# Summing a graph layer's edges on 64-row tiles: six edges in a row on a partition instead of three

## The reference

```python
agg = segment_sum(edge_attr, dst, num_segments=6250)     # (6250, 128)
h   = relu(concat([x, agg, u[0]]) @ W1 + b1)              # (6250, 256)
y   = x + (h @ W2 + b2 + x)
out = layernorm(y)                                        # (6250, 128)
```

## Time and profile before

| | us |
|---|---|
| median of 3 runs | 177.22 (176.80 to 177.23) |
| the profiled execution, its own time | 177.16 |
| span of the profile | 175.4 |
| PE busy / its share of the span | 150.3 / 86% |
| DVE busy / share | 119.8 / 68% |
| ACT busy, POOL busy | 52.8, 34.3 |
| mean rate of the DMA engines | 354 GB/s over 62.07 MB |
| mean granted clock of PE | 0.991 of full speed |

### The profile page before, as it was taken

How to read it: one execution, slowest core, us unless ns; L and a number is a source line. 1 busy time by engine, 2 the same in 40 slices (tenths; PEclk the granted TensorE clock), 3 DMA queues, 4 the chain that set the end, 5 groups by cost and what they waited for, 6 DMA issues and landing times.

```text
span 175.4 us, 5350 instructions
## 1 busy us (share of the span) xinstructions
PE 150.3 (86%) x2191; PEld 113.1 (64%) x2191; DVE 119.8 (68%) x352; ACT 52.8 (30%) x109; POOL 34.3 (20%) x40
## 2 busy tenths in 40 slices
PE   0054799999999999997996999999989999999960
PEld 0044576866796786864774675976845976887840
DVE  5754388988586797766676462797875675685552
ACT  2002242334431430432330423224304305214430
POOL 7900030424120020020020020110200200019350
PEclk9999999999999999999999999999999999999996
DMA  4999999999999999999999999999999999999941
GB/s 110 302 371 382 377 382 376 371 384 372 372 383 373 372 384 371 373 381 375 369 381 374 379 376 372 380 374 374 378 375 373 375 370 371 373 372 384 371 178 37
DMA packets 42244, 62.07 MB, mean 354 GB/s; under 512 B 2023, under 2 KB 39589, under 8 KB 42218
## 3 DMA queue, kind: packets, MB, share of 16 engines
q1 hardware_dynamic: 41094, 61.23, 98.8%
q10 hardware_dynamic: 1124, 0.48, 1.2%
HBM read 58.50 MB, written 3.20 MB: 352 GB/s over the span
## 4 chain that ended last, share of the span: by engine, by line
PE 64%; DMA 23%; DVE 7%; ACT 2%; issue 2%; SPq 0%; DVEq 0%
PE sum_ps L903 22%; DMA edge_ring<-in_edge_attr_dram 20%; PE out_ps L995 9%; PE hid_ps L963 9%; PE hid_ps L976 8%; PE turn_ps L923 7%; DMA base_row<-in_dst_dram 3%; PE xt_ps L941 2%; DVE bases L640 2%; PE hid_ps L995 1%; PE keep_ps L976 1%; PE keep_ps L949 1%; DVE local_rows L648 1%; DVE agg_t L702 1%; ACT local_t L512 1%
## 5 line engine op out<-in xcount | busy, mean ns | idle before, releaser
L903 PE MATMUL sum_ps<-edge_ring,onehot 128*32 128x128 f32 x1662 | 56.7, 280 | 6.5 <-DMA edge_ring<-in_edge_attr_dram 4.2
L903 PEld LDWEIGHTS sum_ps<-edge_ring,onehot 128*32 128x32 f32 x1662 | 43.9, 111 | 14.8 <-DMA edge_ring<-in_edge_attr_dram 6.8
L702 DVE TENSOR_TENSOR agg_t<-agg_t,turn_ps 128x112 f32 x70 | 19.0, 272 | 42.5 <-PE turn_ps L923 38.1
L666 DVE TENSOR_TENSOR onehot<-iota,local_t 128x768 f32<-128x768 f32 (+1 forms) x37 | 42.2, 1142 | 2.4 <-ACT local_t L512 2.4
L469 POOL TENSOR_TENSOR x_all<-x_all,half_b 128x512 f32<-128x512 f32 (+3 forms) x16 | 18.0, 1136 | 113.4 <-PE xt_ps L941 113.4
L524 ACT COPY sums<-sum_ps 128x256 f32<-128x256 f32 (+2 forms) x37 | 13.3, 360 | 61.7 <-PE sum_ps L903 61.7
L923 PEld LDWEIGHTS turn_ps<-place,sums 128*128 128x128 f32 (+1 forms) x140 | 20.2, 191 | 11.1 <-issue 9.1
L923 PE MATMUL turn_ps<-place,sums 128*128 128x112 f32 (+1 forms) x140 | 21.4, 273 | 1.1 <-ACT sums L524 1.1
L976 PE MATMUL hid_ps<-agg_t,w_a 128*128 128x512 f32 (+1 forms) x48 | 22.0, 581 | 0.0
L995 PE MATMUL out_ps<-w_sb,hid_t 128*128 128x128 f32 x160 | 20.4, 281 | 0.0
L995 PEld LDWEIGHTS out_ps<-w_sb,hid_t 128*128 128x128 f32 x160 | 18.7, 191 | 1.8 <-issue 1.8
(11 more groups left out here) (78 smaller groups left out, 91.0 us busy)
## 6 DMA issues: line engine op xcount, KB each, us to landing
edge_ring<-in_edge_attr_dram SPq DMA_DIRECT2D x69, 768.0 KB, 12.0
x_all<-in_x_dram SPq DMA_DIRECT2D x10, 256.0 KB, 10.8
out_dram<-x_all SPq DMA_DIRECT2D x1, 2304.0 KB
dst_rows<-in_dst_dram SPq DMA_DIRECT2D x1, 384.0 KB
x_all<-in_x_dram SPq DMA_DIRECT2D x3, 128.0 KB, 10.9
out_dram<-x_all SPq DMA_DIRECT2D x3, 128.0 KB
out_dram<-x_all SPq DMA_DIRECT2D x1, 256.0 KB
w_x<-in_L_gnn_W_dram ACTq DMA_DIRECT2D x1, 128.0 KB, 6.1
```

Source lines behind the costliest of these rows:

```text
L666: nc.vector.tensor_tensor(onehot[0:ROWS, b % BUFFERS, 0:k * TILES], cols, loc, ALU.is_equal).then_inc(onehot_ready, 1)
L702: nc.vector.tensor_tensor(to, to, turn_ps[:, i * SPAN:(i + 1) * SPAN], ALU.add).then_inc(group_added, 1)
L903: last = nc.tensor.matmul(bank[c * WIN:(c + 1) * WIN], onehot[0:p, b % BUFFERS, i * TILES + c * R + r], edge_ring[0:p, slot, c * R + r], s ...
```

## The change

A partition now holds R = 6 edges in a row, and a window of 384 edges lies on one half of the partitions (64). A group is two blocks s of 128 partitions; the half h of block s is a window. The load of a group moves 256 runs of 3072 bytes. The one-hot matrices are the same in number and size. A sum is now a product over 64 rows: twice as many matmuls, each on a tile of 64 rows and 32 columns of PE. In the second group of a pair the two windows of a block go to swapped places (`to_swapped` gives the offsets to match), so that the two row halves which use the same column tile belong to different groups, and `sum_ps` has a bank for each group of the pair. The matmuls of both groups of a pair are issued in turn. All batches are pairs (35). The second bank comes from `keep_ps`, of which one is left: C_'s product with x is now kept in `x_hid_late` too, and the four products are made one after another in steps 5 to 8. The last pieces' outputs, norms and roots stand in another order.

```diff
-R = 3
+R = 6
 C = 4
-ROWS = 128
-TILES = C * R
+HALF = P // 2
+SUPER = 2
+TILES = SUPER * R
-EDGES_WIN = R * ROWS
+EDGES_WIN = R * HALF
-COMPLETE_AT = [6, 12, 18, 24, 30, 36, 40, 46, 52, 58, 60, 64, 66, 67, 68]
-SINGLE0 = 66
+COMPLETE_AT = [6, 12, 18, 24, 30, 36, 40, 46, 52, 58, 60, 64, 66, 68, 68]
-LATE_SUM_STEP = [5, 6, 7]
+LATE_SUM_STEP = [5, 6, 6, 7, 8]
...
-        sum_ps = psum("sum_ps", [P, BLOCK])
+        sum_ps = psum("sum_ps", [P, PAIR, BLOCK])
-        keep_ps = [psum(f"keep_ps{m}", [P, BLOCK]) for m in range(m_chunks)]
+        keep_ps = psum("keep_ps", [P, BLOCK])
...
-                    sp.dma_start(edge_ring[0:ROWS, slot].rearrange("p (c r) f -> p c (r f)", c=C),
+                    sp.dma_start(edge_ring[:, slot].rearrange("p (s r) f -> p s (r f)", s=SUPER),
                                  edges[g * EDGES_GRP:(g + 1) * EDGES_GRP, :]
-                                 .rearrange("(c p r) f -> p c (r f)", c=C, p=ROWS)).then_inc(...)
+                                 .rearrange("(s p r) f -> p s (r f)", s=SUPER, p=P)).then_inc(...)
...
+            nc.gpsimd.tensor_copy(by_swapped[:, :, 0], by_window[:, :, 1])
+            nc.gpsimd.tensor_copy(by_swapped[:, :, 1], by_window[:, :, 0]).then_inc(consts_ready, 1)
...
-                nc.scalar.copy(sums[0:w, b % 2, 0:k], sum_ps[0:w, 0:k * d].rearrange("s (k f) -> s k f", k=k)
-                               ).then_inc(batch_copied, 1)
+                if b < n_batch - 1:
+                    nc.scalar.copy(sums[:, b % 2], sum_ps[:, :, 0:d]).then_inc(batch_copied, 1)
+                    return
+                nc.scalar.copy(sums[:, b % 2, 0], sum_ps[:, 0, 0:d])
+                nc.scalar.copy(sums[0:WIN, b % 2, 1], sum_ps[0:WIN, 1, 0:d]).then_inc(batch_copied, 1)
...
             relu(END)
-            root(E)
-            root(END)
+            for n in range(C_, n_pieces):
+                root(n)
...
-            norm_step(E, 3)
-            norm_step(E, 4)
-            for step in range(5):
+            for step in range(3):
+                norm_step(ODD, step)
+            norm_step(C_, 3)
+            for step in range(3):
+                norm_step(E, step)
+            norm_step(ODD, 3)
+            for step in range(3):
                 norm_step(END, step)
+            for n in (E, END):
+                norm_step(n, 3)
+                norm_step(n, 4)
...
-            nc.tensor.matmul(out_ps[:, spread_at], to_window[:], rel_t[:, 0:n_grp], start=True,
+            nc.tensor.matmul(out_ps[:, win_at], to_window[:], win_row[:], start=True, stop=True)
+            nc.tensor.matmul(out_ps[:, spread_at], to_window[:], rel_t[:, 0:n_grp], start=True, stop=True)
+            nc.tensor.matmul(out_ps[:, swapped_at], to_swapped[:], rel_t[:, swapped], start=True,
                              stop=True).then_inc(rel_spread, 1)
...
-            def sum_group(b, i, g):
-                slot, bank = g % SLOTS, sum_ps[:, i * d:(i + 1) * d]
-                pe.wait_ge(edges_landed[slot], 16 * (g // SLOTS + (1 if g < full_grp else rest_wins + 3)))
-                for r in range(R):
-                    for c in range(C if g < full_grp else last_wins):
-                        ...
-                        last = nc.tensor.matmul(bank[c * WIN:(c + 1) * WIN],
-                                                onehot[0:p, b % BUFFERS, i * TILES + c * R + r],
-                                                edge_ring[0:p, slot, c * R + r],
-                                                start=(r == 0), stop=(r == R - 1))
-                last.then_inc(group_summed, 1)
+            def sum_window(b, i, g, s, h, r, p):
+                slot, rows_h = g % SLOTS, slice(h * HALF, h * HALF + p)
+                place_at = 2 * s + (h if i == 0 or g == full_grp else 1 - h)
+                return nc.tensor.matmul(sum_ps[place_at * WIN:(place_at + 1) * WIN, i, 0:d],
+                                        onehot[rows_h, b % BUFFERS, i * TILES + s * R + r],
+                                        edge_ring[rows_h, slot, s * R + r],
+                                        start=(r == 0), stop=(r == R - 1))
+
+            def sum_batch(b):
+                pe.wait_ge(onehot_ready, b + 1)
+                for g in groups(b):
+                    pe.wait_ge(edges_landed[g % SLOTS], 16 * (g // SLOTS + (1 if g < full_grp else 3)))
+                whole = [g for g in groups(b) if g < full_grp]
+                for r in range(R):
+                    for s in range(SUPER):
+                        for h in range(2):
+                            for i, g in enumerate(whole):
+                                last = sum_window(b, i, g, s, h, r, HALF)
+                                if (r, s, h) == (R - 1, SUPER - 1, 1):
+                                    last.then_inc(group_summed, 1)
+                if b == n_batch - 1:
+                    for r in range(R):
+                        last = sum_window(b, 1, full_grp, 0, 0, r, rest_rows + (r < rest_tiles))
+                    last.then_inc(group_summed, 1)
...
-            def sum_x_kept():
-                pe.wait_ge(x_t_ready, turned_at[A] + 1)
-                for m in range(m_chunks):
-                    nc.tensor.matmul(keep_ps[m][:, 0:2 * half], w1_x[:, m * P:(m + 1) * P], x_t_late[:, part_cols(0)],
-                                     start=True, stop=True).then_inc(late_x_summed, 1)
+            def sum_x_kept(k, m):
+                pe.wait_ge(x_t_ready, turned_at[late_parts[k][0]] + 1)
+                if k + m > 0:
+                    pe.wait_ge(late_x_kept, m_chunks * k + m)
+                cols = part_cols(0) if k == 0 else late_cols(C_)
+                nc.tensor.matmul(keep_ps[:, 0:cols.stop - cols.start], w1_x[:, m * P:(m + 1) * P], x_t_late[:, cols],
+                                 start=True, stop=True).then_inc(late_x_summed, 1)
...
+            sum_out(ODD)
             sum_hidden_a(END)
+            sum_out(E)
             sum_out(END)
```

More of the change, by code:

```diff
@@ L103, in gnn_resnorm_kernel @@
     pool_scaled = range(LAST, E)
-    assert all(a < b for a, b in zip(hidden_step, hidden_step[1:])) and hidden_step[END] == n_batch
+    assert all(a <= b for a, b in zip(hidden_step, hidden_step[1:])) and hidden_step[END] == n_batch
     made_by = [min(b + 3 + sum(hidden_step[n] <= b for n in range(AHEAD - 2)), n_batch) for b in range(n_batch)]
@@ L180, in gnn_resnorm_kernel @@
         x_t_late = sb("x_t_late", [P, n_nodes - late0])
-        x_hid_late = sb("x_hid_late", [P, m_chunks, 2 * half])
+        x_hid_late = sb("x_hid_late", [P, m_chunks, 3 * half])
         hid_t = sb("hid_t", [P, 2, m_chunks, BLOCK])
@@ L211, in hidden_bank @@
                 return hid_ps[m][:]
-            bank, at = {A: (hid_ps[0], 0), B: (hid_ps[1], 0), C_: (keep_ps[0], 0), ODD: (xt_ps, 0),
-                        E: (keep_ps[1], 0), END: ((xt_ps, 2 * P), (keep_ps[1], P))[m]}[n]
+            bank, at = {A: (hid_ps[0], 0), B: (hid_ps[1], 0), C_: (hid_ps[0], 0), ODD: (xt_ps, 0),
+                        E: (keep_ps, 0), END: ((xt_ps, 2 * P), (keep_ps, P))[m]}[n]
             return bank[:, at + m * p * j:at + (m + 1) * p * j]
@@ L511, in _ @@
                 t1 = min(t0 + per_bank, TILES)
-                last = nc.scalar.copy(lt[0:ROWS, t0:t1],
-                                      ps[0:ROWS, 0:(t1 - t0) * n_grp].rearrange("p (t g) -> p t g", g=n_grp))
+                last = nc.scalar.copy(lt[:, t0:t1],
+                                      ps[:, 0:(t1 - t0) * n_grp].rearrange("p (t g) -> p t g", g=n_grp))
                 t0 = t1
@@ L517, in copy_batch @@
             def copy_batch(b):
-                k = len(groups(b))
                 act.wait_ge(group_summed, batch_first[b + 1])
@@ L540, in copy_x_t, with keep_chunk @@
                 last.then_inc(x_t_ready, 1)
-            def keep_chunk(m):
-                act.wait_ge(late_x_summed, m + 1)
-                nc.scalar.copy(x_hid_late[:, m], keep_ps[m][:, 0:2 * half]).then_inc(late_x_kept, 1)
+            def keep_chunk(k, m):
+                act.wait_ge(late_x_summed, m_chunks * k + m + 1)
+                cols = part_cols(0) if k == 0 else late_cols(C_)
+                nc.scalar.copy(x_hid_late[:, m, cols], keep_ps[:, 0:cols.stop - cols.start]).then_inc(late_x_kept, 1)
             def relu(n):
@@ L780, in _ @@
                     check(3)
-                for n in (A, B):
+                for n in (A, B, C_):
                     if hidden_step[n] == b:
@@ L920, in turn_batch @@
                     pe.wait_ge(group_added, batch_first[b])
-                w = C * WIN if b < n_batch - 1 else last_wins * WIN
-                for i in range(len(groups(b))):
+                for i, g in enumerate(groups(b)):
+                    w = C * WIN if g < full_grp else WIN
                     last = nc.tensor.matmul(turn_ps[:, i * SPAN:(i + 1) * SPAN], sums[0:w, b % 2, i],
@@ L1062, in _ @@
                         pe.wait_ge(gen_added, nb)
```

(2 more changed lines are left out.)

96 lines of the change are left out of this document (46 added, 50 removed).

## The result

The changed kernel takes 209.73 us (median of 4 runs, 207.67 to 211.08) against 177.01 us for the kernel before beside it: 1.182 times as long (95% interval 1.178 to 1.185). The ratio is taken from the three runs that count as undisturbed; the fourth, 211.08 us, was a slow one. The forecast was 174.2 us. The profiled execution took 207.67 us, its span is 205.9 us.

A forecast was written before the change was run, and what follows sets the result against it. PE was taken to bound the first half, with edges just too late from 79 us. Terms -5.3 + 1.7 + 0.5 + 0.9 - 0.8 = -3.0 us against 177.16 gave 174.2 us; own range 171.5 to 176.6, whole range 171 to 196.

The forecast's parts named there:

- the later start of tiles 5 to 8: Sum matmuls: tiles keep 12 matmuls each, only four more starts add 0.05 us per pair, +1.7 us (0 to 3.4).
- Rival B: Sum matmuls: PE can't be fed fast enough; 194 us at 20 ns each, some 206 at 25 ns; chance 0.18.
- Rival A: Sum matmuls: the row halves don't work beside each other, +1.3 us a pair, +44 us, 217 us; chance 0.17.
- The transfers: Edge loads: 3072-byte runs reach 415 GB/s, so all 7 PE waits for edges go, -5.3 us (0 to -5.3).
- Rival C: Edge loads: long runs gain nothing, edges arrive as now, 177.2 us; chance 0.12.
- The prologue: Before the first sum: two more PE products ahead of the transposes, in the open, +0.5 us (0.4 to 1.0).
- Kept products: Step 6: with one bank left, the second product waits for the first's latency and ACT's copy, +0.9 us (0 to 1.8).
- tail: End of the kernel: last groups as pairs, no late one-hot matrices, new order of outputs and norms, together -0.8 us.

The follow-up runs named there:

- run with 128 rows: Changed kernel with each sum product over all 128 rows on four column tiles, 48 matmuls a pair (sums not the reference's): 172.85 us, ratio 0.980.
- tail run: Kernel before with only the changed kernel's end: last groups in pairs, one kept bank, new order of roots and norms: 177.49 us, ratio 1.0039.

## Why the prediction was wrong, by its steps

**The step that failed** is the sum's pace. The forecast added only "the later start of tiles 5 to 8", +1.7 us, for 96 matmuls and 96 weight loads instead of 48 each. That term was right for a pair that isn't interrupted, and missed what lies ahead of PE: its instructions come by DMA, beside the edges. Rival B had the place (PE can't be fed) and not the mechanism: it expected a slower pace, 2.1 us for each pair. What happened is full pace and then a stop of 0.4 to 2.9 us at the end of a block: 21.8 us in 15 stops inside the pairs. The row that would have told it stands in the page of before, `q8 instruction: 18, 0.29, 0.7%`: a share of nothing, but 18 packets for one engine's program, each of which PE needs in time.

**Row halves.** The timeline of an undisturbed pair, weight loads and matmuls:

```profile
96.18 1.32 PEld L921 LDWEIGHTS sum_ps<-edge_ring,onehot 64*32 64x32 f32 x96
96.18 1.59 PE L921 MATMUL sum_ps<-edge_ring,onehot 64*32 64x128 f32 x96
```

1.59 us for 96 on eight tiles, against 1.52 for 48 on four: +0.07 each, 34 x 0.07 = 2.4 us (forecast 1.7). Rival A is out. The Trainium skill's rule that different row tiles can't use one PSUM bank at the same time (TensorEngine Tiling (Array Packing), Restrictions and Gotchas) isn't borne out here: both halves wrote to both banks, and the pair took 1.59 us, not the 2.8 of A. Nor is its floor of 25 ns from start to start (TensorE: Matmul & The Clock Gate, Part 1) for matmuls on different tiles: the 96 start within 1.32 us (1.59 less the 0.27 us of the last one), 13.9 ns each.

**The transfers.** Forecast -5.3. The run with 128 rows gained 3.6 us (2.4 to 4.7) in spite of the prologue (+1.2) and the tail run's +0.7: -3.6 - 1.2 - 0.7 = -5.5 against the tail run, which waited 4.8 us for edges; against the kernel before, with 4.2 us of such waits, it is some -4.9. Both agree with the forecast within the run's interval. The rate was 394 to 400 GB/s in full stretches, not 415; it was enough. Rival C is out.

**The prologue.** Forecast +0.5 (0.4 to 1.0); the first sum starts at 16.73 instead of 15.53, +1.2. `rel` comes 0.3 us later, and the two products' four instructions took 0.9 us.

**Kept products and tail.** The new wait of 0.8 us is there (forecast 0.9, from the copy of the earlier trace rows). The tail was to gain 0.8 us. With the old layout the two together and 0.6 us more waiting for edges came to +0.7, so it gained next to nothing: 0.67 us at the last scaling, given back behind it by POOL (which the forecast named as what "may come to be the last") and by SP's stores, which it didn't name. The last batch's 60 matmuls took 2.74 us in the chain (forecast 2.8).

**What it adds up to.** Without the supply: -5.5 + 2.4 + 1.2 + 0.7 = -1.2 us, some 176 us. The other 34 us are the supply's. Against the run with 128 rows the span is 34.8 us longer: 22.8 us more of issue waits (24.9 against 2.1) and 12.2 us more of busy PE (161.9 against 149.7). The trace divides the latter. 2.3 us are 0.07 in each of 33 pairs, and 0.5 us the last batch with its 60 matmuls. 6.3 us stand in 18 of the pairs, which were busy for 1.82 to 2.17 us instead of 1.59: 15 of them hold a stop, whose last matmul's 0.27 us counts as busy with nothing beside it, and three hold a shorter break, as the pair of 1.81 us above. 3.1 us are in PE's other products, mostly in the two stretches at half clock: a hidden product took 3.36 us at 151 us instead of 1.98, one of half the columns 2.07 us at 185 us instead of 1.13.

**Where the view misled.** The chance of A and B together was 0.35 and the range ended at 196 us, below B's own 25 ns price of 206. The forecast's own range, 171.5 to 176.6 us, isn't the sum of its bounds either: added up they give 171.1 to 183.3. Even that doesn't reach 209.7, as no term stood for the supply. A supply that fails in bursts doesn't show in a kernel that stays within it.

## What to carry to other kernels

Before an edit that multiplies an engine's instructions, count them: the packets of the instruction queue, and how much of the engine's work a block of 256 holds. Here, beside a full load on the DMA engines, 7.9 to 8.5 us of work in a block (medians, counted without the stops) met no stop, 5.8 us cost 6% and 4.9 us 18%; with the DMA engines a quarter busy 4.8 us met none. If the engine that grows is the bound and the transfers fill the DMA engines, gains in the pace of single instructions are lost to the blocks; "issue" idle time inside a run of like instructions, at even distances in the stream, is the mark.

## What the runs showed of the hardware that I had not expected

PE's program came in packets of 16384 bytes during the run, 18 to 31 of them, one for each 256 instructions. One page of the Trainium skill (Trainium Architecture — The Big Picture, The software stack) has the streams moved into the engine's memory when the program is loaded; the packets in these traces, spread over the run, say that it isn't all.

The first instruction of a late block ran 1.2 to 1.6 us after its packet had landed, in all seven kernels with stops. From a block's first matmul to the next packet's start (medians up to 150 us): 0.7 us with the DMA engines at a share of 0.18 to 0.28, 2.6 to 3.9 us at a full share, whatever the packet's length (65 or 121 ns), and 2.7 us with one load in flight at a mean share of 0.57; single ones up to 8 us.

A 3072-byte packet took 121 ns (median) to 128 partitions and some 230 ns where a load filled only 64 of them; the rate fell from 394 to some 190 GB/s with the DMA engines still 0.80 to 0.89 busy.
